# Vision-tower kernel: decay rows fetched through device memory, one wide power split in two, and the output transposes and first masked level moved in the order

## The reference

```python
q = _l2norm(_silu(q_c)); k = _l2norm(_silu(k_c)); v = _silu(v_c)
alpha = jax.nn.sigmoid(_linear(x, Wa, ba))[..., 0]
beta = jax.nn.sigmoid(_linear(x, Wb, bb))[..., 0]
...
Sk = jnp.einsum('bij,bj->bi', St, kt)
Sn = a * (St - b * Sk[:, :, None] * kt[:, None, :]) + b * vt[:, :, None] * kt[:, None, :]
ot = jnp.einsum('bij,bj->bi', Sn, qt)
...
gdn = _zc_rmsnorm(gdn, norm_w)
gate = _silu(_linear(x, Wg, bg))
return _linear(gdn * gate, Wo, bo)
```

## Time and profile before

| What | Value |
|---|---|
| Median of three runs | 891.03 us (890.76 to 892.22) |
| The profiled execution | 895.05 us |
| Its span, first to last instruction | 893.2 us |
| PE busy | 838.4 us, 94% |
| DVE busy | 664.9 us, 74% |
| ACT busy | 482.1 us, 54% |
| POOL busy | 355.4 us, 40% |

### The profile page before, as it was taken

One profiled execution on the slowest core, in us unless ns is written; L12 is line 12 of the kernel. 1 busy time (PEld: TensorE's weight loads), 2 busy tenths in 40 slices (PEclk: granted clock), 3 DMA queues, 4 the chain that ended last, 5 costly groups with the idle time before them and its releaser, 6 DMA issues. The chain is left out here.

```text
span 893.2 us, 31060 instructions
## 1 busy us (share of the span) xinstructions
PE 838.4 (94%) x11766; PEld 634.7 (71%) x11766; DVE 664.9 (74%) x2420; ACT 482.1 (54%) x1721; POOL 355.4 (40%) x530
## 2 busy tenths in 40 slices
PE   5689999999999999999999999999985999999996
PEld 2357777777777777777777777777764677777775
DVE  3466888888888888888888888888764676868434
ACT  0434455565655565565655565566523355666654
POOL 3122333233332332233332332333211178888875
PEclk9999999999999999999999999999958799999999
...
DMA packets 78659, 45.33 MB, mean 51 GB/s; under 512 B 20357, under 2 KB 69803, under 8 KB 78511
## 3 DMA queue, kind: packets, MB, share of 16 engines
...
q10 hardware_dynamic: 848, 0.54, 0.2%
...
## 5 line engine op out<-in xcount | busy, mean ns | idle before, releaser
L1050 PE MATMUL bank<-SA,work 128*128 128x386 f32 x200 | 93.5, 550 | 6.5 <-ACT work L528 6.5
L1647 PEld LDWEIGHTS bank<-work 128*128 128x128 f32 x768 | 89.6, 192 | 12.5 <-issue 12.5
L1529 ACT ACTIVATE work<-bank,b1mix 128x512 f32<-128x512 f32 x96 | 66.0, 687 | 59.4 <-PE bank L1621 59.3
L438 ACT ACTIVATE logit<-bank 128x2 f32<-128x2 f32 x100 | 17.3, 173 | 149.3 <-PE bank L1051 149.1
L1647 PE MATMUL bank<-work 128*128 128x128 f32 x768 | 89.9, 275 | 0.8 <-DVE work L1407 0.8
L616 POOL TENSOR_SCALAR var2e<-mv 128x4 f32<-128x4 f32 x25 | 5.7, 227 | 211.1 <-DVE mv L795 211.1
L1621 PE MATMUL bank<-work 128*128 128x512 f32 x192 | 86.5, 593 | 0.0
L1051 PE MATMUL bank<-SB,work 128*128 128x256 f32 x200 | 60.8, 386 | 0.0
L1621 PEld LDWEIGHTS bank<-work 128*128 128x128 f32 x192 | 34.6, 190 | 34.6 <-issue 34.4
L1010 PEld LDWEIGHTS bank<-work 32*32 32x32 f32 x3200 | 35.6, 108 | 32.9 <-issue 27.2
L1051 PEld LDWEIGHTS bank<-SB,work 128*128 128x128 f32 x200 | 38.9, 194 | 27.9 <-issue 1.8
...
## 6 DMA issues: line engine op xcount, KB each, us to landing
hn_kept<-work SPq DMA_DIRECT2D x25, 256.0 KB, 2.3
hnT_kept<-work SPq DMA_DIRECT2D x25, 256.0 KB, 2.3
work<-hnT_kept SPq DMA_DIRECT2D x25, 256.0 KB, 2.9
work<-hn_kept SPq DMA_DIRECT2D x25, 256.0 KB, 3.1
out_dram<-work SPq DMA_DIRECT2D x24, 256.0 KB, 2.5
tv<-in_L_ffn_tv_W_dram SPq DMA_DIRECT2D x16, 256.0 KB
work<-r_kept SPq DMA_DIRECT2D x25, 98.0 KB
...
```

The costliest lines, as they stand in the source:

```text
L1050: mm(t[:, 0:386], xs[p][:, b, HIST:XW], SA[:, 0:386], start=True, stop=False)
L1529: ins = nc.scalar.activation(hid[f][:, :], ps[:, :], ACT.Relu, bias=b1mix[:, of[0], f:f + 1])
L1647: ins = mm(by4(bank[2 + par])[:, t, :], hid[f][:, t * C:(t + 1) * C], w2T[of[t]][:, f, :], start=(f == 0 and t == 0), stop=(f == FB - 1), ...
```

## The change

It does five things. The alpha rows no longer come from four PE transposes. They stand beside the norm factors in one tile `to_rows`, one transpose makes eight rows, and one write to device memory takes both. A new DMA copies the alpha rows over 128 partitions into `arows`, ahead of the `rrows` reads on SP. The scan reads `arows`. The power of eight numbers becomes two of four, alpha first. On DVE the key norm goes ahead of `o`, `xs` goes ahead of the scan, and `og` goes behind level 0 and `Pm`. The four output transposes and their ACT copy move into the next iteration, behind level 1, and the output product behind the second key-value product. The residual addition on DVE moves behind `grow(1)`.

The core of the diff (first the constants and SP, then ACT, POOL, DVE, PE):

```diff
-        r_dram = nc.dram_tensor("r_kept", (STEPS, NB, C), F32).ap()
+        r_dram = nc.dram_tensor("r_kept", (STEPS + 1, 2 * NB, C), F32).ap()
...
+        arows = tile(NB * C)
...
+        to_rows = sb("to_rows", [D, 2 * NB])
+        rstd1 = to_rows[:, 0:NB]
...
+        ab0 = to_rows[:, NB:2 * NB]
...
+                i = j - first
+                if on(j, LE) or on(j, LF):
+                    sp.wait_ge(r_row_ready, i + 1)
+                    sp.dma_start(r_dram[i], rrows[64:64 + 2 * NB, 0, :]).then_inc(r_out, 16)
+                    sp.wait_ge(r_out, 16 * (i + 1))
+                if on(j, LF):
+                    need(sp, decay_ready, j + LF)
+                    sp.dma_start(arows, r_dram[i, NB:2 * NB].rearrange("b t -> (b t)").partition_broadcast(D)).then_inc(arows_in, 16)
                 if on(j, LE):
                     s = j + LE
-                    sp.wait_ge(r_row_ready, s + 1)
-                    sp.dma_start(r_dram[s], rrows[64:64 + NB, 0, :]).then_inc(r_out, 16)
-                    sp.wait_ge(r_out, 16 * (s + 1))
                     if s == 0:
                         sp.wait_ge(rrows_set, 1)
                     need(sp, xs_ready, s)
-                    sp.dma_start(rrows[0:PIX + 1], r_dram[s].partition_broadcast(PIX + 1)).then_inc(rrows_in, 16)
-                    sp.dma_start(rrows[PIX + 2:KX], r_dram[s:s + 1]).then_inc(rrows_in, 16)
+                    sp.dma_start(rrows[0:PIX + 1], r_dram[i, 0:NB].partition_broadcast(PIX + 1)).then_inc(rrows_in, 16)
+                    sp.dma_start(rrows[PIX + 2:KX], r_dram[i:i + 1, 0:NB]).then_inc(rrows_in, 16)
                 if on(j, LH):
...
                 kvg_out(0)
+                if on(j, LH):
+                    s = j + LH
+                    act.wait_ge(ogT_ps, s + 1)
+                    need(act, wo_ps, s)
+                    nc.scalar.copy(ogT, by4(bank[7])).then_inc(ogT_ready, 1)
                 kvg_out(1)
...
                     nc.scalar.activation(qT[p], by4(bank[4]), ACT.Silu).then_inc(qT_ready, 1)
-                if on(j, LE):
-                    s = j + LE
-                    act.wait_ge(r_row_ps, s + 1)
-                    need(act, r_out, 16 * s)
-                    if s == 0:
+                if on(j, LE) or on(j, LF):
+                    i = j - first
+                    act.wait_ge(r_row_ps, i + 1)
+                    need(act, r_out, 16 * i)
+                    if i == 0:
...
-                    nc.gpsimd.tensor_tensor(expo[:, :], euler[:, :], logit[:, :], ALU.pow).then_inc(expo_ready, 1)
+                    nc.gpsimd.tensor_tensor(expo[:, 0:NB], euler[:, 0:NB], logit[:, 0:NB], ALU.pow).then_inc(expo_ready, 1)
+                    need(pool, beta1_ready, s)
+                    nc.gpsimd.tensor_tensor(expo[:, NB:], euler[:, NB:], logit[:, NB:], ALU.pow).then_inc(expo_b_ready, 1)
+                    pool.wait_ge(expo_b_ready, s + 1)
...
-                if on(j, LH):
-                    s = j + LH
-                    h = h1buf[:, :, bass.ds(s, 1), :].rearrange("p b s c -> p b (s c)")
-                    dve.wait_ge(wo_ps, s + 1)
-                    dve.wait_ge(h0_kept, s + 1)
-                    nc.vector.tensor_tensor(h, by4(bank[6]), h, ALU.add).then_inc(h1_ready, 1)
                 new_blocks(1)
...
                 grow(1)
+                if on(j, LH):
+                    s = j + LH
+                    h = h1buf[:, :, bass.ds(s, 1), :].rearrange("p b s c -> p b (s c)")
+                    dve.wait_ge(wo_ps, s + 1)
+                    dve.wait_ge(h0_kept, s + 1)
+                    nc.vector.tensor_tensor(h, by4(bank[6]), h, ALU.add).then_inc(h1_ready, 1)
...
                     need(dve, ab_ready, s)
-                    nc.vector.tensor_scalar(expo1[:, :], expo[:, :], 1.0, None, ALU.add).then_inc(expo1_ready, 1)
+                    nc.vector.tensor_scalar(expo1[:, 0:NB], expo[:, 0:NB], 1.0, None, ALU.add).then_inc(expo1_ready, 1)
                     dve.wait_ge(expo1_ready, s + 1)
                     need(dve, glast_ready, s)
-                    nc.vector.reciprocal(ab[:, :], expo1[:, :]).then_inc(ab_ready, 1)
+                    nc.vector.reciprocal(ab[:, 0:NB], expo1[:, 0:NB]).then_inc(ab_ready, 1)
                     dve.wait_ge(ab_ready, s + 1)
-                    need(dve, alpha_ps, s)
-                    nc.vector.tensor_tensor(ab0[:, :], ab[:, 0:NB], not_first[:, :], ALU.mult).then_inc(ab0_ready, 1)
+                    need(dve, r_row_ps, j - first)
+                    nc.vector.tensor_tensor(ab0, ab[:, 0:NB], not_first[:, :], ALU.mult).then_inc(ab0_ready, 1)
                 if on(j, LI):
...
                 grow(4)
+                if on(j, LF):
+                    s = j + LF
+                    dve.wait_ge(expo_b_ready, s + 1)
+                    need(dve, beta_ready, s)
+                    nc.vector.tensor_scalar(expo1[:, NB:], expo[:, NB:], 1.0, None, ALU.add).then_inc(beta1_ready, 1)
+                    dve.wait_ge(kvg_ready, NB * (s + 1))
+                    dve.wait_ge(ssk_ready, s + 1)
+                    need(dve, rk2_ready, s)
+                    need(dve, knorm_ready, s)
+                    nc.vector.tensor_scalar(kn2[:, :], ssk[:, :], 1e-24, None, ALU.max).then_inc(kn2_ready, 1)
+                    dve.wait_ge(beta1_ready, s + 1)
+                    need(dve, cneg_ready, s)
+                    nc.vector.reciprocal(ab[:, NB:], expo1[:, NB:]).then_inc(beta_ready, 1)
+                    dve.wait_ge(kn2_ready, s + 1)
+                    nc.vector.reciprocal(rk2[:, :], kn2[:, :]).then_inc(rk2_ready, 1)
+                    dve.wait_ge(rk2_ready, s + 1)
+                    dve.wait_ge(beta_ready, s + 1)
+                    need(dve, cdecay_ready, s)
+                    nc.vector.scalar_tensor_tensor(cneg[:, :], rk2[:, :], -1.0, ab[:, 4:8], ALU.mult, ALU.mult).then_inc(cneg_ready, 1)
...
+                if on(j, LF):
+                    s = j + LF
+
+                    dve.wait_ge(arows_in, 16 * (s + 1))
+                    need(dve, g_out, 16 * s)
+                    need(dve, cdecay_ready, s)
+                    nc.vector.tensor_tensor_scan(decay.rearrange("p b c -> p (b c)"), arows,
+                                                 ident4[:, :, :].rearrange("p b c -> p (b c)"), 0.0, ALU.mult, ALU.add).then_inc(decay_ready, 1)
+                    dve.wait_ge(decay_ready, s + 1)
+                    nc.vector.tensor_copy(glast[:, NB:2 * NB], ab[0:1, 0:NB])
+                    nc.vector.tensor_tensor(glast[:, 0:NB], decay[0:1, :, C - 1], ab[0:1, 0:NB], ALU.mult).then_inc(glast_ready, 1)
...
                     nc.vector.tensor_tensor(Pm[p], by4(bank[3]), cdecay, ALU.mult).then_inc(P_ready, 1)
+                if on(j, LC):
+                    s = j + LC
+                    dve.wait_ge(oscale_ready, s + 1)
+                    dve.wait_ge(kvg_ready, NB * (s + 1))
+                    need(dve, ogT_ps, s)
+                    for b in range(NB):
+                        nc.vector.scalar_tensor_tensor(og[:, b, :], o[:, b, :], oscale[:, b:b + 1], kvg[s % 3][:, b, 2 * D:3 * D],
+                                                             ALU.mult, ALU.mult).then_inc(og_ready, 1)
...
-                        if E_:
-                            pe.wait_ge(r_row_ready, e + 1)
-                        if C_:
-                            need(pe, ogT_ready, c)
+                        if E_ or F_:
+                            pe.wait_ge(r_row_ready, j - first + 1)
+                        need(pe, ogT_ready, h + 1)
...
                 level_update(1)
+                if H_:
+                    need(pe, ogT_ready, h)
+                    need(pe, blk_ready, 6 * min(s0, STEPS))
+                    for b in range(NB):
+                        pe.wait_ge(og_ready, NB * h + b + 1)
+                        ins = tr(by4(bank[7])[:, b, :], og[:, b, :], ident[:, :])
+                    ins.then_inc(ogT_ps, 1)
...
+                if H_:
+                    pe.wait_ge(ogT_ready, h + 1)
+                    need(pe, hnT_ready, h)
+                    need(pe, o_ready, h + 1)
+                    for b in range(NB):
+                        ins = mm(by4(bank[6])[:, b, :], ogT[:, b, :], Wo_T[:, :], start=True, stop=True)
+                    ins.then_inc(wo_ps, 1)
...
-                if E_:
-                    pe.wait_ge(rstd1_ready, e + 1)
-                    need(pe, ogT_ready, c)
-                    tr(bank[7][0:NB, 0:C], rstd1[:, :], ident[:, :]).then_inc(r_row_ps, 1)
+                if E_ or F_:
+                    if j == first:
+                        pe.wait_ge(rrows_set, 1)
+                    if E_:
+                        pe.wait_ge(rstd1_ready, e + 1)
+                    if F_:
+                        pe.wait_ge(ab0_ready, s1 + 1)
+                    need(pe, ogT_ready, h + 1)
+                    tr(bank[7][0:2 * NB, 0:C], to_rows[:, :], ident[:, :]).then_inc(r_row_ps, 1)
                 level_blocks(4)
...
-                if F_:
```

(13 more changed lines are left out.)

95 lines of the change are left out of this document (32 added, 63 removed).

## The result

The changed kernel takes 938.94 us (931.45 to 950.9), beside 891.62 us of the kernel before on the same chip: 1.0493 times as long, 95% interval 1.046 to 1.0526. The profiled execution took 942.5 us with a span of 940.7. The chain of reasons ran in the right direction and ended 41.5 us too low. The direction hung on little: without the 0.25 us for the DMAs its sum for an iteration was -0.08 us.

What follows compares the result with a forecast made beforehand. A loop of PE's head and DVE's tail was taken to bound the kernel. Per iteration -1.76 + 1.67 + 0.25 = +0.16 us, times 21 = +3.4, plus ends +3, gave +6.4 on 891.03: 897.4 us, range 885 to 914.

Steps and rivals of the forecast that it cites:

- The loop of head and tail: Each iteration: PE's work limits level 1 to level 5 (16.07 us), DVE's list limits from there to next level 1 (9.10).
- PE's tail becomes the bound: Rival: no `rrows` wait and a shorter DVE tail let PE limit both parts; iteration 24.73 us, 885 us; chance 0.20.
- Into PE's head: Between level 1 and level 5: output transposes, output product and a mask 0.20 us late add 1.67 us per iteration.
- Out of DVE's tail: After level 5: gating (1.17 us) and key norm (0.59) leave DVE's list, saving 1.76 us per iteration.
- The transposed rows: PE's transpose of eight columns now needs alpha too; alpha comes about 0.64 us earlier, so no wait and no cost.
- The DMAs: On SP, `rrows` may queue behind `arows`; DVE then waits 0 to 0.5 us per iteration, taken as 0.25.
- the DMAs queue: Rival: `arows` streams slowly at 97 GB/s, DVE waits 1.6 us more per iteration; +34 us, 931 us; chance 0.11.
- The late return of the write: The write of the rows returning late would delay `rrows` as slow `arows` does, at a smaller price; expected return 1.19 us.
- The ends: First gated chunk about +3 us, iteration 1 -1.4, iteration 24 about +2, iteration 25 about -0.7; together +3, between 0 and +6.
- POOL holds the scan: Rival: the scan, reading SBUF twice, waits for POOL's output-scale power, up to 1.0 us per iteration; 918 us; chance 0.03.

Runs made afterwards that it cites:

- kn_only: The kernel before with only the split power, the split sigmoid and the key norm ahead of `o`; 878.12 us, ratio 0.9828.
- alpha_pe_qm2: alpha_pe with the query-state product moved from PE's head to ahead of level 1, and the scan directly behind `xs`; 892.21 us, ratio 0.9992.
- alpha_pe: The changed kernel with the alpha rows made by four PE transposes again, everything moved stays moved; 909.98 us, ratio 1.0173.
- after_once: The changed kernel with the alpha rows copied once, before the loop, not in each iteration; 911.0 us, ratio 1.0216.
- before_trip2: The kernel before with a second small write to device memory, waited for, ahead of the `rrows` reads; 892.77 us, ratio 1.0003.

## Why the prediction was wrong, step by step

- **The loop of head and tail** held. kn_only, which shortens DVE's tail only, becomes faster until PE has no gap, at 24.69 us. That is the rival "PE's tail becomes the bound", but in the kernel without the moved products, so that its 24.73 is near by chance. With them it came true only in alpha_pe_qm2.
- **Into PE's head, +1.67.** Measured +1.72 (17.79 against 16.07), with the 0.20 us wait for the mask as worked out. Right.
- **Out of DVE's tail, -1.76.** Without a wait for rows it is -1.34 in alpha_pe; in the changed kernel 8.31 - 0.72 = 7.59 us against 9.10, -1.51. Gating and key norm left the tail as said. What the step left out is that `ovar` and `qn2e`, at their new place, stand between `xs` and the scan and wait for ACT and for each other. That is 0.31 of the 0.42 us in alpha_pe, but only 0.05 of the 0.25 in the changed kernel, where the rest stays open. Mis-sized by 0.25 to 0.42 us per iteration, 5 to 9 us in all.
- **The transposed rows** don't wait (L1145 has no idle time noted). Right.
- **The DMAs, 0.25 per iteration.** This is the step that failed. I took 2.3 us for `arows` from a copy in the other direction; it takes 3.4. The normal wait is 0.72 to 1.0 and not 0.25. And the step left no cover for a late write, at no cost, which is the next point. The rival "the DMAs queue" named this mechanism, with a price of 1.6 us more per iteration where normal ones show 0.47 to 0.75 more, and I held it at 0.11 on the ground that 128 partitions use more DMA engines. after_once shows its worth: between 100 and 640 us `xs` waits 4 times without the copy and 20 times with it, and the kernel takes 28 us less.
- **The late return of the write** stands in the rival as "acts the same way at a smaller price". The old trace had some, and I read the earlier trace rows alone: four of its 25 writes took over 1.4 us. The longest, on SP in the kernel before:

```profile
410.36 0.27 SPq L395 DMA_DIRECT2D r_kept<-work  x1
412.32 0.27 SPq L400 DMA_DIRECT2D work<-r_kept  x1
```

  No row showed a wait for it, since the cover was 2 us by the prediction's sum; before_trip2 shows that 1.2 of them were there. A cover that is taken away must be held against the longest return and not against the median. In the changed kernel the returns are later still, up to 3.57 us, which no row of before showed.
- **PE's clock** had no term. Each long wait of DVE for `rrows` is one of PE, and behind the longest the granted clock is 0.83 where it was 1.00, that is, PE spends part of the stretch at 1.2 GHz. Together with the late returns this is the 22.5 us beyond 21 normal iterations, about 13 of them slower products. Not each of these iterations has a late write: that from 197.84 has a return of 1.23 us, a wait of 1.77 and a clock of 0.88. after_once, with late writes and no copy, keeps its clock, and its 21 iterations cost 12.1 us, of which 21 times 0.43 are 9.0 and 3.1 are the longer ones. So it is the copy in front of `rrows` that made late writes dear.
- **The ends, +3.** Measured 5.65 at the start and -1.25 behind the last full iteration, +4.4 together, inside 0 to +6. That is luck: the start was put at +3 and came out 2.6 us higher, the end was put at +1.3 and came out 2.5 us lower. An end also differs by some 2.5 us between executions, as before_trip2 shows.
- **POOL holds the scan, 0.03.** It doesn't: the scan from 507.94 takes 1.22 us as it did from PSUM, and POOL's power for the scale runs from 507.84 to 508.85:

```profile
507.84 1.01 POOL L665 TENSOR_TENSOR oscale<-ovar,half_neg 128x4 f32<-128x4 f32 x1 [1.75 <-issue]
```

  The rule of the Trainium skill (SBUF — State Buffer, "Who interferes with whom") on the pair of ports that DVE and GpSimd share would keep the two apart; by these rows it does not here (starts and lengths on POOL are rough in a profile).

In the sum for a normal iteration: 0.16 predicted, +0.47 for the wait (0.72 for 0.25), +0.05 for the head and +0.25 for the tail make 0.93, where 0.93 to 0.98 was measured. Times 21 that is up to 20.6 of the 43.1 us, half of it the wait. The other half is late returns and the clock, which had no term and no place in the range.
